# Layernorm's two small steps on another engine, and new instruction orders behind the attention slots

## The reference

```python
def _layernorm(x, axis=-1, eps=1e-05):
    m = jnp.mean(x, axis=axis, keepdims=True)
    v = jnp.var(x, axis=axis, keepdims=True)
    return (x - m) / jnp.sqrt(v + eps)
x = x + attn_a(_layernorm(x), ...)   # 16 heads of 64, causal, output product Wo and bias bo
x = x + ffn(_layernorm(x), ...)      # relu(x w1 + b1) w2 + b2, 512 wide
x = x + attn_b(_layernorm(x), ...)   # one head of 128, causal, with a linear position bias
x = x + ffn(_layernorm(x), ...)      # the same weights again
```

## Time and profile before

| | |
|---|---|
| median of 3 runs | 575.68 us (575.47 to 575.82) |
| the profiled execution | 579.0 us, its span 577.0 us |
| PE busy | 528.2 us (92%) |
| PEld busy | 369.8 us (64%) |
| DVE busy | 444.7 us (77%) |
| ACT busy | 468.5 us (81%) |
| POOL busy | 455.8 us (79%) |
| granted clock of PE, mean | 0.988 |

### The profile page before, as it was taken

One profiled execution on the slowest core, in us unless ns is written; L12 is line 12 of the kernel. 1 busy time (PEld: TensorE's weight loads), 2 busy tenths in 40 slices (PEclk: granted clock), 3 DMA queues, 4 the chain that ended last, 5 costly groups with the idle time before them and its releaser, 6 DMA issues.

```text
span 577.0 us, 17876 instructions
## 1 busy us (share of the span) xinstructions
PE 528.2 (92%) x6844; PEld 369.8 (64%) x6844; DVE 444.7 (77%) x1383; ACT 468.5 (81%) x923; POOL 455.8 (79%) x446
## 2 busy tenths in 40 slices
PE   4688999899999999999999999997988998788886
PEld 3445666566676667666766667664788795546664
DVE  5588888788888888888888888887776575689822
ACT  3659889889988999899989999889873869473983
POOL 5658899678888888888888888896965956564995
PEclk9989999999999999999999999999989999899999
DMA  9423334232433333423334243358108000000001
GB/s 230 113 56 72 85 86 111 56 94 58 119 84 94 93 76 102 104 74 96 80 104 110 56 121 77 100 141 319 39 38 292 2 3 2 1 1 2 1 20 55
DMA packets 36435, 48.54 MB, mean 84 GB/s; under 512 B 10728, under 2 KB 17792, under 8 KB 36352
## 3 DMA queue, kind: packets, MB, share of 16 engines
q1 hardware_dynamic: 34240, 46.88, 29.6%
q10 hardware_dynamic: 2112, 0.54, 0.4%
HBM read 12.79 MB, written 9.44 MB: 39 GB/s over the span
## 4 chain that ended last, share of the span: by engine, by line
PE 65%; ACT 10%; DVE 9%; issue 8%; POOL 7%; DMA 1%; POOLq 0%; ACTq 0%; DVEq 0%
PE psum L555 9%; PE psum L611 9%; PE psum L612 9%; PE psum L509 6%; PE psum L511 6%; PE psum L510 6%; PE psum L591 5%; PE psum L593 5%; PE psum L592 5%; PE psum L614 2%; ACT xn L1130 2%; ACT p_hl L1202 2%; POOL h_lo L2077 2%; POOL p_hlb L2084 2%; POOL p_hl L2004 2%
## 5 line engine op out<-in xcount | busy, mean ns | idle before, releaser
L2004 POOL TENSOR_TENSOR p_hl<-p,p_hl 128x512 f16<-128x512 f32 x288 | 327.4, 1162 | 54.0 <-ACT p_hl L1202 50.6
L1481 DVE CUSTOM_DVE_ANT_0 max_junk<-psum,mask_s 128x1024 bf16<-128x1024 f32 (+7 forms) x256 | 190.2, 753 | 32.0 <-issue 31.8
L1201 ACT ACTIVATE p<-psum 128x512 f32<-128x512 f32 x288 | 178.2, 619 | 16.4 <-PE psum L614 14.1
L1202 ACT ACTIVATE p_hl<-psum 128x512 f16<-128x512 f32 x288 | 179.6, 624 | 0.0
L591 PE MATMUL psum<-v_all,p_hl 128*128 128x65 f16 x1152 | 125.5, 193 | 1.7 <-POOL p_hl L2004 1.7
L611 PE MATMUL psum<-q_hl,k_hh 128*128 128x512 f16 (+3 forms) x384 | 125.1, 326 | 1.4 <-ACT p_hl L1202 1.4
L592 PE MATMUL psum<-v_all,p_hl 128*128 128x64 f16 x1152 | 125.6, 193 | 0.0
L593 PE MATMUL psum<-v_all,p_hl 128*128 128x65 f16 x1152 | 125.2, 194 | 0.0
L612 PE MATMUL psum<-q_hm,k_l 128*128 128x512 f16 (+3 forms) x384 | 121.8, 326 | 0.0
L591 PEld LDWEIGHTS psum<-v_all,p_hl 128*128 128x128 f16 x1152 | 107.4, 98 | 16.7 <-POOL p_hl L2004 1.8
L592 PEld LDWEIGHTS psum<-v_all,p_hl 128*128 128x128 f16 x1152 | 106.7, 97 | 4.9
(11 more groups left out here) (205 smaller groups left out, 1109.1 us busy)
## 6 DMA issues: line engine op xcount, KB each, us to landing
k_hh<-st_hi SPq DMA_DIRECT2D x64, 128.0 KB, 2.3
o_scratch<-o_sb SPq DMA_DIRECT2D x16, 512.0 KB, 2.6
o_in<-o_scratch SPq DMA_DIRECT2D x4, 2048.0 KB, 10.5
k_l<-st_lo SPq DMA_DIRECT2D x32, 128.0 KB, 2.3
q_hl<-st_hi SPq DMA_DIRECT2D x32, 128.0 KB, 2.3
q_hl<-st_lo SPq DMA_DIRECT2D x32, 128.0 KB, 2.3
q_hm<-st_hi SPq DMA_DIRECT2D x32, 128.0 KB, 2.3
x_sb<-in_L_attn_a_x SPq DMA_DIRECT2D x4, 256.0 KB, 3.7
```

Source lines behind the costliest of these rows:

```text
L1201: nc.scalar.activation(p32[:, ring_at(u, r), :], src, ACT.Exp, scale=SCALE_A).then_inc(exp_done, 1)
L1202: nc.scalar.activation(p_hl[:, u % 2, 0, BANK * r:BANK * (r + 1)], src, ACT.Exp, scale=SCALE_A).then_inc(phi_done, 1)
L1481: nc.vector.tensor_tensor_reduce(out=max_junk[:, n % 2, 0:cols], in0=max_banks(v, j, 0, cols), in1=mask_s[:, S - cols:S], scale=1.0, scala ...
L2004: nc.gpsimd.tensor_tensor(p_hl[:, u % 2, 1, cols], p32[:, ring_at(u, r), :], p_hl[:, u % 2, 0, cols], ALU.subtract)\
```

## The change

Two edits. First, `var_eps` (add eps) moves for all 16 chunks, and the negation of the mean for the 14 late ones, from POOL's `chunk_rstd` and `chunk_shift` to the end of DVE's `chunk_stats`, behind a wait for its own `bn_aggr`:

```diff
@@ DVE, chunk_stats
                 last.then_inc(aggr_done, 1)
+                dve.wait_ge(aggr_done, n + 1)
+                cols = slice(CT * c, CT * (c + 1))
+                nc.vector.tensor_scalar(var_eps[:, cols], mean_var[:, cols, 1], EPS, None, ALU.add).then_inc(eps_done, 1)
+                if n >= LATE_CHUNKS[0]:
+                    nc.vector.tensor_scalar(shift[:, cols], mean_var[:, cols, 0], -1.0, None, ALU.mult).then_inc(mean_turned, 1)
@@ POOL, chunk_rstd
-                pool.wait_ge(aggr_done, n + 1)
-                nc.gpsimd.tensor_scalar(var_eps[:, cols], mean_var[:, cols, 1], EPS, None, ALU.add).then_inc(eps_done, 1)
                 pool.wait_ge(eps_done, n + 1)
                 nc.gpsimd.tensor_tensor(rstd[:, cols], var_eps[:, cols], minus_half[:, :], ALU.pow).then_inc(rstd_done, 1)
@@ POOL, chunk_shift
-                nc.gpsimd.tensor_scalar(shift[:, cols], mean_var[:, cols, 0], -1.0, None, ALU.mult).then_inc(mean_turned, 1)
                 pool.wait_ge(mean_turned, n - LATE_CHUNKS[0] + 1)
```

Second, the lists of PE, ACT, DVE and POOL behind the slots hold the same calls in another order (some 200 moved lines). The places that the prediction speaks of (PE's first, DVE's and POOL's after it):

```diff
@@ PE, first lines
             turn_block(0, 2)
+            turn_block(0, 3)
             outputs(HEADS - 1, 0)
+            turn_block(0, 4)
             outputs(HEADS - 1, 1)
-            turn_block(0, 3)
-            turn_block(0, 4)
             turn_block(0, 5)
...
+            turn_block(0, 7)
             outputs(HEADS - 1, 5)
-            turn_block(0, 7)
+            outputs(HEADS - 1, 6)
             turn_block(1, 0)
-            outputs(HEADS - 1, 6)
-            turn_block(1, 1)
             outputs(HEADS - 1, 7)
             outputs(HEADS - 1, 8)
+            turn_block(1, 1)
             output_tile(0, 0)
@@ PE, before scores_b(0, 0)
+            max_tile_b(0, 7)
+            turn_maxima_b(0)
             forward(3, 2)
             forward(3, 3)
-            max_tile_b(0, 6)
-            max_tile_b(0, 7)
-            turn_maxima_b(0)
             scores_b(0, 0)
@@ DVE, first lines
             tail_norm()
-            tail_gain()
             outputs_out(HEADS - 2, 0)
             outputs_out(HEADS - 2, 1)
+            tail_gain()
             block_low(0, 0)
@@ DVE, around max_rows_b(0)
             take_max_b(0, 6)
             take_max_b(0, 7)
+            add_result(7, 0)
+            max_rows_b(0)
+            add_result(7, 1)
             late_stats(ln_of[2, 3])
-            max_rows_b(0)
@@ DVE, around late_stats(3, 0)
+            outputs_out_b(0, 2)
+            max_rows_b(1)
             outputs_out_b(0, 3)
-            max_rows_b(1)
+            outputs_out_b(0, 4)
+            biased(1, 0)
             late_stats(ln_of[3, 0])
-            biased(1, 0)
-            outputs_out_b(0, 4)
             biased(1, 1)
@@ POOL, first lines
-            tail_root()
             low(HEADS - 1, 0)
             low(HEADS - 1, 1)
             low(HEADS - 1, 2)
+            tail_root()
             low(HEADS - 1, 3)
             low(HEADS - 1, 4)
             low(HEADS - 1, 5)
-            add_output_row(0)
             low(HEADS - 1, 6)
             low(HEADS - 1, 7)
             low(HEADS - 1, 8)
-            add_output_row(1)
-            add_output_row(2)
+            add_output_row(0)
@@ POOL, around rstd of chunk (3, 0)
+            low_b(1, 0)
             late_rstd(ln_of[3, 0])
-            low_b(1, 0)
-            add_forward_row(4)
             low_b(1, 1)
             low_b(1, 2)
             low_b(1, 3)
+            add_forward_row(4)
             low_b(1, 4)
```

More of the change, by code:

```diff
@@ L941, in _ @@
             output_tile(0, 1)
-            output_tile(0, 2)
             turn_block(1, 5)
             turn_block(1, 6)
+            output_tile(0, 2)
             turn_block(1, 7)
@@ L968, in _ @@
             output_tile(2, 1)
+            turn_block(3, 2)
             hidden(1, 0)
@@ L978, in _ @@
             turn_block(3, 3)
+            forward(0, 2)
+            forward(0, 3)
             turn_block(3, 4)
             turn_block(3, 5)
[L981 to L984, removed]
             forward(1, 0)
             forward(1, 1)
+            turn_block(3, 6)
             forward(1, 2)
+            turn_block(3, 7)
+            forward(1, 3)
             turn_late(ln_of[1, 2])
-            forward(1, 3)
             output_tile(3, 0)
-            turn_late(ln_of[2, 0])
             output_tile(3, 1)
             output_tile(3, 2)
+            turn_late(ln_of[2, 0])
+            hidden(2, 0)
+            hidden(2, 1)
             output_tile(3, 3)
@@ L996, in _ @@
             turn_late(ln_of[2, 1])
-            hidden(2, 0)
-            hidden(2, 1)
+            hidden(2, 2)
+            hidden(2, 3)
             values_b(0)
-            hidden(2, 2)
             queries_b(1)
             turn_late(ln_of[1, 3])
-            hidden(2, 3)
             max_tile_b(0, 0)
-            values_b(1)
[L1006 to L1011, removed]
+            forward(2, 0)
+            forward(2, 1)
+            forward(2, 2)
+            max_tile_b(0, 1)
+            hidden(3, 0)
+            forward(2, 3)
+            hidden(3, 1)
+            max_tile_b(0, 2)
+            hidden(3, 2)
+            values_b(1)
             hidden(3, 3)
-            max_tile_b(0, 2)
-            forward(2, 2)
-            forward(2, 3)
             max_tile_b(0, 3)
+            max_tile_b(0, 4)
+            max_tile_b(0, 5)
             forward(3, 0)
-            max_tile_b(0, 4)
+            max_tile_b(0, 6)
             forward(3, 1)
-            max_tile_b(0, 5)
+            max_tile_b(0, 7)
+            turn_maxima_b(0)
             forward(3, 2)
             forward(3, 3)
-            max_tile_b(0, 6)
-            max_tile_b(0, 7)
-            turn_maxima_b(0)
             scores_b(0, 0)
@@ L1091, in _ @@
             hidden(6, 1)
+            forward(5, 0)
             hidden(6, 2)
-            forward(5, 0)
             forward(5, 1)
+            forward(5, 2)
+            hidden(6, 3)
             turn_late(ln_of[3, 3])
-            hidden(6, 3)
-            forward(5, 2)
             forward(5, 3)
@@ L1101, in _ @@
             hidden(7, 2)
+            forward(6, 0)
             hidden(7, 3)
-            forward(6, 0)
             forward(6, 1)
@@ L1304, in _ @@
             exponentials(HEADS - 1, 6)
-            tail_high(0)
+            exponentials(HEADS - 1, 7)
             block_high(0, 0)
@@ L1813, in _ @@
             block_low(2, 0)
+            tail_low(3)
             block_low(2, 1)
@@ L1820, in _ @@
             block_low(2, 7)
+            block_low(3, 0)
             chunk_low(ln_of[1, 1])
-            block_low(3, 0)
+            block_low(3, 1)
             add_result(2, 0)
-            block_low(3, 1)
             add_result(2, 1)
@@ L1827, in _ @@
             block_low(3, 2)
+            block_low(3, 3)
             add_result(3, 0)
-            block_low(3, 3)
-            block_low(3, 4)
-            block_low(3, 5)
             add_result(3, 1)
             late_stats(ln_of[2, 0])
+            block_low(3, 4)
             add_result(4, 0)
+            block_low(3, 5)
             block_low(3, 6)
@@ L1837, in _ @@
             add_result(4, 1)
+            late_stats(ln_of[2, 1])
             chunk_low(ln_of[1, 2])
-            late_stats(ln_of[2, 1])
+            chunk_low(ln_of[2, 0])
             add_result(5, 0)
-            chunk_low(ln_of[2, 0])
             add_result(5, 1)
@@ L1899, in _ @@
             biased(1, 3)
+            biased(1, 4)
+            biased(1, 5)
             outputs_out_b(0, 6)
-            biased(1, 4)
             outputs_out_b(0, 7)
+            biased(1, 6)
             late_stats(ln_of[3, 1])
-            biased(1, 5)
-            biased(1, 6)
+            biased(1, 7)
             chunk_low(ln_of[3, 0])
-            biased(1, 7)
             outputs_out_b(1, 0)
+            biased(1, 8)
             outputs_out_b(1, 1)
-            biased(1, 8)
             outputs_out_b(1, 2)
@@ L1918, in _ @@
             outputs_out_b(1, 7)
+            late_stats(ln_of[3, 3])
             chunk_low(ln_of[3, 2])
             add_result(8, 0)
-            late_stats(ln_of[3, 3])
             add_result(8, 1)
```

173 lines of the change are left out of this document (85 added, 88 removed).

## The result

The changed kernel took 586.19 us (median of 6 executions, 581.99 to 588.04), the kernel before 576.81 us beside it (6, 575.47 to 579.67): a ratio of 1.015 with a 95% interval of 1.0105 to 1.0195. The forecast was 577.3, with a range of 572.5 to 581.5. Its sign holds; its size does not, and the time lies outside the range. The profiled execution took 586.73 us, its span 584.9.

A forecast was written before the change was run, and what follows sets the result against it. PE was taken to bound the slots, then DVE (516 to 528 us) and POOL (528 to 549), the waits running through POOL's layernorm. Terms summed to +1.6 on a median of 575.7: 577.3 us, 8-in-10 range 572.5 to 581.5.

The forecast's parts named there:

- the clock, inside "The middle": 486 to 528 us: if the clock stays up, 6 us at 0.51 shrink to 3; half of that counted as gain.
- What leaves POOL: Layernorm chunks: eps and negation leave POOL, 0.62 us per late chunk at five chunks; -2.9, and -0.2 at the kernel's start.
- In the slots: Slots 1 and 2: new DVE instructions wait for POOL's low parts, delaying the st_lo that PE waits for; +4.4.
- The new order, entry: 417 to 430 us: later tail_root and tail_gain make PE stand, POOL's second wait goes; +1.3, bounds -1.0 and +3.9.
- the pause in "The middle": 486 to 528 us: PE's 2.0 us wait for max_rows_b(0) loses 1.5, with forward(3,2) and forward(3,3) under it.
- chunk (3,0): Late layernorm chunk: eps meets a running low part, with biased(1,1) behind it; +1.2, bounds -1.0 and +2.2.
- chunks (3,1) to (3,3): Late layernorm chunks: they meet a busy POOL, up to 2.2 us each on DVE; +0.8, bounds 0 and 3.
- the level it was added to: Whole kernel: starting time of 575.7 us, the runs' median, to which the sum of +1.6 was added.
- No half-clock stretch behind `max_rows_b(0)`: The middle: a sign that would show the prediction right; PE still at half clock there would show it wrong.
- Rival 3: Attention slots: pauses there lower PE's clock, adding 3.4 us for 580.7; chance 0.11.
- rival 1: Slots 1 and 2: the new DVE pairs miss POOL and cost 0.3 us each instead of 2.2, giving 573.5; chance 0.21.
- the prediction's +1.0: Chunk (3,0): by the page's rule the negation would also wait for POOL's power instruction, +1.0 at that one place.

The follow-up runs named there:

- a1_move_only: The kernel before with only the first edit: eps and negation on DVE (VectorE), every list in its old order; 580.85 us, ratio 1.0055.
- b4_clock_fill: The changed kernel plus 76 extra unused products on PE around the maxima of the second batch; 582.99 us, ratio 1.0116 to the kernel before.
- b2_entry_slots: The changed kernel with tail_root and tail_gain at their old places and eps and negation of chunks 2 and 3 on POOL; 575.56 us, ratio 0.9982.
- c3_before_fill: The kernel before plus extra unused PE products, 12 ahead of turn_maxima_b(0) and 34 behind it; 576.56 us, ratio 0.9995.
- a5_entry: The changed kernel with only tail_root and tail_gain back at their old places in POOL's and DVE's lists; 578.93 us, ratio 1.0037 to the kernel before.
- d1_stats_first: b2_entry_slots with late_stats(3,0) on DVE and late_rstd(3,0) on POOL back at their earlier places; ratio 0.9984 to the kernel before.

## Why the prediction was wrong, step by step

The miss is 586.2 - 577.3 = 8.9 us by the medians. By the means it is 8.4, of which 7.0 are terms and the rest the level that they were added to.

| step | forecast | measured | from |
|---|---|---|---|
| the clock, inside "The middle" | -1.5 | +4.0 | mean clock over 6 executions, and the line |
| "What leaves POOL" | -3.1 | -0.3 | rest of `a1_move_only` (+2.2) less the slots |
| "In the slots" | +4.4 | +2.5 | slots 1 and 2 |
| "The new order, entry" | +1.3 | +3.2 | first `output_tile`, after against before |
| the pause in "The middle", chunk (3,0), chunks (3,1) to (3,3) | +0.5 | -0.8 | what is left of after's rest of +4.6 |
| sum | +1.6 | +8.6 | the means |
| the level it was added to | 575.7 | 577.2 | median of 82 instead of 3 |

The last term is a remainder, so the sum comes out by itself. The sign of the forecast came true with the two losses that it did foresee, slots and entry.

**The step that failed most: the clock.** "If the clock stays up, the 6 us at 0.51 shrink to 3", and half of that was booked as gain. "No half-clock stretch behind `max_rows_b(0)`" came true and the wait of 2.0 for `qm_b` went. But the gain was reckoned as if all else would stay at full clock. After has three new stretches, each behind pauses of PE, and its mean clock is lower by 0.0099, which is +4.0 us by the line. The runs bear out part of that as a cause: keeping the clock up behind 522 (`b4_clock_fill`) gives back 2.8 in the means. And 2.6 goes by itself when entry and slots are mended (`b2_entry_slots`), so it is a consequence of those two; why the other 1.4 stays is open. Rival 3 had the clock falling in the slots, where it did not: pauses of 1.48 us there lowered nothing (granted clock 1.00 from 50 to 76). Nor was the pause itself worth 1.5: from `max_rows_b(0)` to `max_rows_b(1)` before takes 25.90 us, but 23.75 with its clock kept up (`c3_before_fill`), and the new order with its clock up there takes 23.88 (`a5_entry`). What looked like a gain to be had from the order was the half clock's 2.15, and in the time of `c3_before_fill` not even that is seen.

**What leaves POOL.** A late chunk takes 1.30 instead of 1.93 us on POOL (528.04 to 529.97 before), as forecast, but that is worth some 0.3 us and not 3.1. The chain of waits was read as if every step on it were won each time that it passes; after the edit it leaves `rstd` altogether, and the tail of `a1_move_only` from `max_rows_b(1)` on is no shorter.

**The entry.** It came out 1.9 us too small, inside its bounds, and both halves of that can be named. The prediction reckoned `tail_gain` from POOL: "It and those three low parts now end at 412.34 + 3 x 1.12", so `tail_gain` from 416.3 to 422.0, which is +9.0 to +14.7 behind the marker. POOL's part was right (`tail_root` ends at +9.04). But it did not go through DVE's own list: `tail_gain` had also been moved behind `outputs_out(30, 1)`, which waits for sums that PE brings only at 419.9, and the 5.04 us of idle DVE are that. So `tail_gain` runs from +10.35 to +15.82, 1.1 us later. The other half is the wait of 0.87 us for `oT_lo` ahead of the first `output_tile`, which was not in the sum. The rest was right: five instructions at a POOL instruction each, 5.47 us in all (5.65 forecast), PE at the end of its third block, POOL's second wait gone. The price of the two moved calls was seen only as part of a net of +1.3; putting them back (`a5_entry`) takes 7.3 us off after, 5.1 of it rest, and that is the largest single loss of the change.

**The slots.** That each of the two instructions is held by one POOL instruction was half right. The first was held in both slots (1.16 and 1.07), so rival 1, a miss by 0.1 us, fell. The second took 0.15. The prediction had read `tail_gain`, where one instruction after another is held; but those wait for each other's result and are issued a little later, when POOL has taken up its next. The negation waits for nothing and follows at once (53.23, where the low part behind the first begins at about 53.27). That this is the reason was not tried apart. The Trainium skill, "SBUF — State Buffer", section "Who interferes with whom", has a `tensor_scalar` contend in a two-port mode and not outside of these; five of 16 wide ones held and none of 64 of one column agree with that. Whether a negation would also wait for the power instruction, the prediction's +1.0, no run shows: each that was not behind a held one had ended when `rstd` began.

**Chunk (3,0) and behind**, +1.2 and +0.8. In the profile eps of chunk (3,0) was not held: it takes 0.17 us at 536.77, and POOL's low part began at 536.87. Held were (3,1) and (3,3), 0.99 and 1.08 us, and no negation, where the forecast had up to 2.2 for each chunk. `d1_stats_first` shows nothing of the 1.2. No run splits the remainder of -0.8 further.

**The size of the clock.** The prediction took 6 us at half clock to be 3 too long. Over a span of 577, 0.001 of mean clock is 1.15 us at the lower level, and it costs 0.40: each microsecond at half clock costs 0.35, not 0.5. PE is not the bound in all of them: against `c3_before_fill` before's profile loses 2.15 us for the stretch behind `max_rows_b(0)` (0.72 over 12 us, so 6.7 at the lower level), and 1.60 for the one at the entry (0.86 over 12, so 3.4). The Trainium skill, "TensorE: Matmul & The Clock Gate", section "Terms", puts the penalty at the throttled time x (1 - K/N), which is half of it at the lower level; here the measurement is lower, and decides.

## What to carry to other kernels

When a call is moved in an in-order list, go through the new list ahead of it, call by call, for what each waits: the time of a moved instruction is set by the last of these as much as by its own operand. A step on the chain of waits is not won as often as the chain passes it: the chain moves elsewhere. Before pricing a stretch at the lower clock from one profile, look at how the clock varies over executions of the same kernel: a stretch that one execution shows may be absent in the next, and removing PE's pause in one place does not keep the clock up where the new order makes other pauses. A small `tensor_scalar` of four columns that begins beside a running POOL instruction cost about one POOL instruction here (0.93 to 1.16 us), and the next right behind it nothing; at a place that PE waits for, leave it on POOL (slots as before), or cut it into single columns (half the loss stays).

## What had not been expected of the hardware

- The mean granted clock of one and the same program varied from 0.982 to 0.997 between executions, and its time with it, 580.6 to 574.6 us: 87% of the variance of its times. The same wait of 1.7 us for POOL at the entry had the half clock behind it in one profile (0.86 from 420 to 432) and not in another (1.00).
- A 128x4 `tensor_scalar` that waits for nothing, right behind a held one on DVE, took 0.15 to 0.16 us all five times, in the slots with two more low parts queued on POOL.
- One column alone does not spare an instruction the wait: `tail_gain`'s `out_scale` (L1673, `tensor_tensor` with both operands in SBUF, 128x1) took 1.19 us beside POOL's low parts in after; its `tensor_scalar` of one column (L1674) took 0.14.
